# Softmax reciprocals brought into the attention's layout by VectorE block turns instead of TensorE transposes

## The reference

```python
x, ctx_1024: (8, 512, 512) float32
# attention, 16 heads of 32 columns, queries from layernorm(x), keys = values = ctx
scores = einsum('bhqd,bhkd->bhqk', qh, kh) / sqrt(32)
scores = where(|q - k| > 64, -inf, scores)        # a band of 64 keys to either side
attn = softmax(scores)
y = einsum('bhqk,bhkd->bhqd', attn, vh)           # heads joined again: (8, 512, 512)
x = x + y @ W_proj.T + b_proj
# gated recurrence over the 8 batch entries, on xn = layernorm(x)
for b in range(8):                                # xt = xn[b]: (512, 512), c: (512, 512)
    f = sigmoid(xt @ wf.T + c @ uf.T + bf)
    i = sigmoid(xt @ wi.T + c @ ui.T + bi)
    g = tanh(xt @ wc.T + c @ uc.T + bc)
    c = f * c + i * g
x = x + tanh(xn @ wo.T + c @ uo.T + bo)           # c of the last step for all b
```

## Time and profile before

| what | value |
|---|---|
| median of 3 runs (lowest, highest) | 1018.29 us (1018.28, 1021.04) |
| the profiled execution | 1014.17 us |
| its span, from first to last instruction | 1012.4 us |
| PE, PEld busy | 986.0 us (97%), 748.4 us (74%) |
| DVE busy | 605.5 us (60%) |
| ACT, POOL busy | 500.8 us (49%), 226.8 us (22%) |

### The profile page before, as it was taken

The page is one execution under the profiler, slowest core; times in us unless marked ns, Lnnn a source line. Parts: engine busy times, 40 slices in busy tenths (PEclk is TensorE's granted clock), DMA queues, the critical chain, the costliest instruction groups (busy, mean ns, idle before and its releaser), DMA issues.

```text
span 1012.4 us, 20358 instructions
## 1 busy us (share of the span) xinstructions
PE 986.0 (97%) x7100; PEld 748.4 (74%) x7100; DVE 605.5 (60%) x2194; ACT 500.8 (49%) x1472; POOL 226.8 (22%) x320
## 2 busy tenths in 40 slices
PE   6998999999999999999999999999999999999997
PEld 4664567777777777777777777777777778888886
DVE  5676887776567755776677656775586532133222
ACT  5767666555555445555455545455455432131221
POOL 4555322211111111211111111111121110002354
PEclk9998999999999999999999999999999999999999
DMA  8355322222222222211222222111111012029666
GB/s 268 123 153 177 110 74 79 84 79 74 80 84 79 74 70 67 71 46 63 78 85 80 73 80 84 58 53 48 61 38 50 11 39 108 0 99 360 247 218 198
DMA packets 76245, 99.37 MB, mean 98 GB/s; under 512 B 5232, under 2 KB 46192, under 8 KB 74608
## 3 DMA queue, kind: packets, MB, share of 16 engines
q1 hardware_dynamic: 75424, 97.80, 30.2%
q10 hardware_dynamic: 720, 0.27, 0.1%
HBM read 68.69 MB, written 29.36 MB: 97 GB/s over the span
## 4 chain that ended last, share of the span: by engine, by line
PE 87%; DMA 5%; DVE 2%; ACT 2%; issue 2%; POOL 1%; SPq 1%; DVEq 0%; POOLq 0%; ACTq 0%
PE ps_g L494 18%; PE ps_g L496 16%; PE ps_g L495 16%; PE ps_a L530 7%; PE ps_a L549 4%; PE ps_v L570 3%; PE ps_m L494 3%; PE ps_m L496 3%; PE ps_m L495 3%; PE ps_m L592 2%; PE ps_v L575 2%; ACT probs L670 1%; PE ps_m L604 1%; DMA keys<-x_dram 1%; PE ps_m L505 1%
## 5 line engine op out<-in xcount | busy, mean ns | idle before, releaser
L767 DVE CUSTOM_DVE_ANT_0 probs<-ps_a,mask 128x192 f32<-128x192 f32 (+1 forms) x512 | 169.5, 387 | 167.8 <-PE ps_a L530 158.8
L670 ACT ACTIVATE probs<-probs,rowmin 128x192 f32<-128x192 f32 (+1 forms) x512 | 239.2, 473 | 1.6 <-DVE rowmin L767 1.6
L712 ACT ACTIVATE gate<-ps_g,bias 128x512 f32<-128x512 f32 x84 | 57.8, 688 | 211.4 <-PE ps_g L496 211.4
L790 DVE STREAM_TRANSPOSE probs_t<-probs 32x128 f32<-32x128 f32 x492 | 146.5, 298 | 6.0
L478 POOL COPY recip<-invsum 128x128 f32<-128x128 f32 x128 | 37.7, 295 | 488.1 <-DVE invsum L774 488.1
L494 PE MATMUL ps_g<-state_hi,gate_w 128*128 128x512 f32 x336 | 138.2, 411 | 0.0
L675 ACT ACTIVATE probs_t<-ps_a 128x512 f32<-128x512 f32 x108 | 64.4, 596 | 147.4 <-PE ps_a L549 146.8
L496 PE MATMUL ps_g<-state_hi,gate_w 128*128 128x512 f32 x336 | 131.4, 391 | 0.0
L495 PE MATMUL ps_g<-state_lo,gate_w 128*128 128x512 f32 x336 | 131.3, 391 | 0.0
L670 ACT ACTIVATION_READ_ACCUMULATOR probs<-probs,rowmin 128x1 f32 x512 | 98.8, 193 | 0.0
L530 PE MATMUL ps_a<-keys,queries 32*128 32x256 f32 (+1 forms) x1024 | 86.2, 407 | 2.1 <-DVE rowmin L767 1.3
(11 more groups left out here) (177 smaller groups left out, 1764.6 us busy)
## 6 DMA issues: line engine op xcount, KB each, us to landing
values<-ctx_rows SPq DMA_DIRECT2D x34, 256.0 KB, 4.3
xr<-x SPq DMA_DIRECT2D x32, 256.0 KB, 3.9
keys<-ctx_t SPq DMA_DIRECT2D x16, 512.0 KB, 4.1
x_dram<-xr SPq DMA_DIRECT2D x32, 256.0 KB, 4.2
gate_w<-x2t_dram SPq DMA_DIRECT2D x8, 1024.0 KB, 10.9
keys<-ctx_t SPq DMA_DIRECT2D x16, 384.0 KB, 3.4
x2t_dram<-x2t_even SPq DMA_DIRECT2D x12, 512.0 KB, 4.0
x2t_dram<-x2t_odd SPq DMA_DIRECT2D x12, 512.0 KB, 3.8
```

Of the source, the lines that this page charges most:

```text
L670: act.activation(row, row, ACT.Exp, bias=rowmin[:, i % 2, h:h + 1], scale=-1.0, accum_out=rowsum[:, i // G % 2, i % G, h:h + 1]).then_inc( ...
L712: act.activation(gate[:, min(gt, 1), :], ps_g[i % 2][:, :], ACT.Tanh, bias=(first_bias if b == 0 else bias)[:, gt, m:m + 1], scale=1.0 if ...
L767: dve.tensor_tensor_reduce(probs[:, i % 2, h, 0:SEEN[t]], ps_a[h][:, 0:SEEN[t]], mask[:, MASK0[t]:MASK0[t] + SEEN[t]], -SCALE, -NEG, ALU.a ...
L790: turn = dve.transpose(probs_t[BLK * keys_of:BLK * (keys_of + 1), HPG:2 * HPG, q], probs[q, i % 2, :, col:col + BLK])
```

## The change

The step `spread` leaves TensorE, GpSimd and ScalarE and becomes VectorE's. For each half tile (two groups) it issues 16 block turns of a repeated column: for each of 4 heads and each of 4 blocks of 32 queries, 32 partitions of `invsum`, a column repeated 32 times for two groups, are turned into 32 partitions of `recip`. The half tile's `spread` stands behind `sides` in the slots with s of 0 and s of 2. `mult` reads `recip` as its second input and takes over two waits that `spread` had brought it before (for `tile_row` being free).

```diff
             if s > 0:
-                tile_steps((None, "query", "turn2", "spread")[s], (None, i + 1, i - 1, i)[s])
+                tile_steps((None, "query", "turn2", None)[s], (None, i + 1, i - 1, -1)[s])
             cells(2)
...
         if early:
-            tile_steps(("proj", "query", "turn2", "spread")[s], (i - 1, i + 1, i - 1, i)[s])
+            tile_steps(("proj", "query", "turn2", None)[s], (i - 1, i + 1, i - 1, -1)[s])
...
             steps.append(("recip", n + 1))
             if n + 1 >= OWN_BANKS:
                 steps.append(("sides", n + 1))
+            if (n + 1) % 2:
+                steps.append(("spread", (n + 1) // 2))
...
-                if kind == "recip":
-                    pool.wait_ge(inverted, i + 1)
-                    need(pool, spread, i // G)
-                    pool.tensor_copy(recip[:, i % G, :].rearrange("p (h d) -> p h d", h=HPG),
-                                     invsum[:, i // G % 2, i % G, :].unsqueeze(2).to_broadcast([P, HPG, HEAD]))\
-                        .then_inc(inv, 1)
...
-                if kind == "spread":
-                    pe.wait_ge(inv, G * (i + 1))
+                if kind == "proj":
                     need(pe, q_ready, min(i + 2, TILES))
                     need(pe, x2_lo, i)
-                    for g in range(G):
-                        mm = pe.transpose(ps_m[:, g * P:(g + 1) * P], recip[:, g, :], ident[:, :])
-                    mm.then_inc(spread, 1)
-                if kind == "proj":
...
-                if kind == "spread":
-                    act.wait_ge(spread, i + 1)
-                    act.activation(attn, ps_m[:, :].rearrange("p (g q) -> p g q", g=G), ACT.Copy).then_inc(recip_out, 1)
...
                 if kind == "recip":
                     r, g = i // G % 2, i % G
                     dve.wait_ge(expd, HPG * (i + 1))
-                    need(dve, inv, i - 2 * G + 1)
+                    need(dve, inv_turned, 2 * (i // G - 1))
                     dve.reciprocal(invsum[:, r, g, :], rowsum[:, r, g, :]).then_inc(inverted, 1)
+                if kind == "spread":
+
+                    tile, g0 = i // 2, 2 * (i % 2)
+                    dve.wait_ge(inverted, 2 * (i + 1))
+                    need(dve, attn_t, tile)
+                    for h in range(HPG):
+                        for c in range(0, P, BLK):
+                            sums = invsum[c:c + BLK, tile % 2, g0:g0 + 2, h:h + 1].to_broadcast([BLK, 2, HEAD])
+                            turn = dve.transpose(recip[HEAD * h:HEAD * (h + 1), g0:g0 + 2, c:c + BLK], sums)
+                    turn.then_inc(inv_turned, 1)
...
                 if kind == "mult":
-                    dve.wait_ge(recip_out, i + 1)
+                    dve.wait_ge(inv_turned, 2 * (i + 1))
                     dve.wait_ge(valued, G * (i + 1))
-                    dve.tensor_tensor(tile_row[:, :], ps_v[:, :], tile_row[:, :], ALU.mult).then_inc(attn_t, 1)
+                    dve.wait_ge(q_turned, min(i + 2, TILES))
+                    need(dve, x2_turned, i)
+                    dve.tensor_tensor(tile_row[:, :], ps_v[:, :], recip[:, :, :].rearrange("p g q -> p (g q)"),
+                                      ALU.mult).then_inc(attn_t, 1)
```

More of the change, by code:

```diff
@@ L290, in bass_xattn_ffn @@
         consts = sem("consts"); rstd1 = sem("rstd1"); rstd2 = sem("rstd2"); xr_ready = sem("xr_ready")
-        inv = sem("inv"); w_lo = sem("w_lo"); summed = sem("summed")
+        w_lo = sem("w_lo"); summed = sem("summed")
         attn_split = sem("attn_split"); wp_lo = sem("wp_lo")
         stat1 = sem("stat1"); aggr1 = sem("aggr1"); var1 = sem("var1"); ln1 = sem("ln1")
-        masked = sem("masked"); inverted = sem("inverted"); turned_b = sem("turned_b"); cleared = sem("cleared")
+        masked = sem("masked"); inverted = sem("inverted"); inv_turned = sem("inv_turned"); turned_b = sem("turned_b"); cleared = sem("cleared")
         attn_t = sem("attn_t"); x1_done = sem("x1_done")
@@ L300, in bass_xattn_ffn @@
         out_lo = sem("out_lo"); emptied_ps = sem("emptied_ps"); last_summed = sem("last_summed")
-        q_ready = sem("q_ready"); expd = sem("expd"); turned_a = sem("turned_a"); recip_out = sem("recip_out")
+        q_ready = sem("q_ready"); expd = sem("expd"); turned_a = sem("turned_a");
         attn_round = sem("attn_round"); wp_hi = sem("wp_hi")
@@ L307, in bass_xattn_ffn @@
         q_turned = sem("q_turned"); scored = sem("scored"); turned = sem("turned"); turned_2 = sem("turned_2"); valued = sem("valued")
-        spread = sem("spread"); projected = sem("projected"); state_used = sem("state_used")
+        projected = sem("projected"); state_used = sem("state_used")
         column = sem("column")
```

## The result

The changed kernel takes 1170.92 us (median of 4 runs, 1169.93 to 1171.87), the kernel before 1018.28 us (4 runs, 1017.36 to 1021.04): a ratio of 1.148, 95% interval 1.145 to 1.152. That is 153 us more, where 64 were forecast, and outside the range of 1041 to 1110. It lies even beyond the highest rival, 1127 us.

The account below looks back on a forecast made before the run. The prediction took TensorE as the bound before, with VectorE's work a floor under each stretch after. It added 15, 18 and 31 us to the profiled 1014.2, giving 1078, plus 4.1 for the runs' median: 1082 us, range 1041 to 1110.

Parts of the forecast that it names:

- the highest rival: Every burst: a turn costs by its count, not its size, 0.316 us, bursts of 5.05 us; 1127 us, chance 0.12.
- VectorE's total: Whole kernel: VectorE busy about 846 us, 79% of the span, with 1024 turns added to about 605 us.
- the worth of TensorE's saving taken alone: Whole kernel: 32 groups of four transposes leave TensorE, worth 14.8 us if TensorE is the bound everywhere.
- the chain through places 2 and 3: Six-cell slots: from place 2's masks to place 3's `value`, VectorE's work plus burst exceeds the time there; +31 us.
- At place 0 the burst lies beside the long projection: Six-cell slots, places 0 and 1: VectorE's lateness is worked off by the end of place 1; no time added.
- Not all of VectorE's waits for results there can be filled: Slots 0 to 19: 3 us of pauses on top of at least 12.3 us more; +15 us.
- some 0.2 us a slot: Slots 20 to 35: this much stays empty between dependent instructions, on top of +14.5 us; +18 us.
- The floors: VectorE's own work as each stretch's least length: 104.1 us in slots 0 to 19, 103.5 us in slots 20 to 35.
- The granted clock reads 1.00 there and 0.96 in slots 0 to 19: First 36 slots, "there" being slots 20 to 35: the clock was given no term, so no time.
- that only the averages count: Six-cell slots absorb the bursts, since a whole entry fits; only the first 36 slots pay; 1041 us, chance 0.14.
- That the load alone counts: Rival in the follow-up runs: only the amount of VectorE's work counts, wherever it stands; 1171 us for late0, no chance given.
- that turns aren't held: Every burst: turns not held up by partition changes, 0.135 us each, bursts of 2.2 us; 1023 us, chance 0.07.

Follow-up runs that it names:

- one_turn: Changed kernel with 15 of each burst's 16 turns left out, the rest of `recip` a constant: 1005.90 us, ratio 0.989 to the kernel before.
- late0: Changed kernel with the burst of place 0 moved behind `ln1b`, `resid` and `stat2` in slots 20 and later: 1118.19 us, ratio 1.098 to the kernel before.
- filled: Changed kernel with idle transposes on TensorE ahead of `value` in slots 0 to 19, where it waits: 1161.22 us, ratio 1.141 to the kernel before.
- late_all: As late0, and in slots 0 to 19 each burst also stands behind the next slot's copy: 1126.8 us, ratio 1.105 to the kernel before.
- wide_turns: Changed kernel with one burst a tile, at place 2, of 16 turns of 32 x 128 taking all four groups: 1135.91 us, ratio 1.116.
- one_block: Changed kernel with eight turns a burst, heads 2 and 3 left out, all reading and writing partitions 0 to 31: 1021.94 us, ratio 1.004.
- sides_first: As late0, with the blends of the gates behind `recip` and `sides` at place 3 of slots 20 and later: 1093.19 us, ratio 1.075.

## Why the prediction was wrong

The sign was right, and so were the price of a turn (0.248 us, bursts of 3.97; 0.248 and 3.98 measured), VectorE's total, the worth of TensorE's saving taken alone (14.8 us, 12 measured, by one_turn) and the chain through places 2 and 3. The four tiles' terms there, +3.1, +1.9, +0.65 and 0, came out as +3.2, +2.4, +1.0 and +0.2 in the entry from 515.94 us on. The six-cell slots miss 56 us, slots 0 to 19 21 us, slots 20 to 35 15 us. Three steps failed.

- *"At place 0 the burst lies beside the long projection, and VectorE's lateness is worked off by the end of place 1."* I walked VectorE's order and compared its lateness at the next masks, and left out that TensorE needs two of VectorE's results in between, though the same text names `query` as waiting for `ln1b` and `resid`. It could be seen in the trace of the kernel before. There `resid` ends at 421.12 us, 5.1 us after the masks' start, and TensorE's `query` starts at 422.47, 6.45 us after it: 1.35 us of slack for a burst of 3.97. That makes 2.6 us of wait, and 2.54 were measured. In the entry from 515.94 us on, places 0 and 1 of the four tiles cost 9.0 us, nothing was forecast. Moving the burst (late0) gave 53 us back. This is the largest part of the miss.
- *"Not all of VectorE's waits for results there can be filled; I take 3 us for those"*, and some 0.2 us a slot for slots 20 to 35. The floors held to 0.1 us in slots 0 to 19 and to 2 us in slots 20 to 35, and the time lay 24 and 21 us above them. In slots 0 to 19, 15.7 of the 23.9 us are waits that stay with the clock at its old value (filled), so the term of 3 us should have been near 16 of the 27 us in which VectorE was idle there. Neither another place (late_all) nor fewer, longer turns (wide_turns) made these slots shorter; the clock was low in both. In slots 20 to 35 late0 took 7 us off, so a third of the pause there came from the burst of place 0.
- *"The granted clock reads 1.00 there and 0.96 in slots 0 to 19, so it is no term here"*. That was the clock of the kernel before. Longer waits of TensorE gave half clock for 53 of the first 140 us. filled puts 8.6 us of slots 0 to 19 on it. In slots 20 to 35 (clock 0.89) its part wasn't separated from that of the waits. Nor do these runs say how much of the 15.7 us that are left in slots 0 to 19 belongs to which wait.

The rivals: that only the averages count (1041 us) is refuted by the entry itself, 127.1 us where the work of VectorE and of TensorE each fit into 109. That the load alone counts, the opposite, is refuted by late0: the same work, 8.7 us less. That a turn costs by its count is refuted by 236 ns against the 303 of wide_turns, and that turns aren't held by the 0.25 us from start to start and by one_block. The rival of 1127 us was nearest in number, but its condition, 0.316 us a turn, wasn't met.

## What to carry to other kernels

An engine at 60% has room for more work only where no other engine comes to wait for what stands behind that work. For each place of a moved block, list every consumer of every instruction behind the block up to the next one, and compare each with the time at which that consumer would be ready; the next wait of the engine itself isn't enough. Where two engines answer each other step by step, the idle time of one is in large part the working time of the other, and little of it can be filled: here 12 of 27 us, with the clock kept up. And where an insertion makes TensorE wait, the clock of the kernel before is no longer the clock of the kernel after.

## What the runs showed of the hardware

- A 32 x 64 float32 block turn starts 0.25 us after the last when it reads other 32 partitions than the last one (every fourth also writes others), 0.13 us after it when all read and write the same ones (one_block); the record of one is 236 and 190 ns long. A change of the output's partitions alone was not tried.
- A repeated column (stride 0) as a turn's input costs nothing that shows: 32 x 128 turns took 303 ns with it and 302 ns without.
- After waits of 2 to 6 us, TensorE's products ran at half clock for stretches. Idle transposes in the waits of slots 0 to 19 kept the clock up (0.96 against 0.79) and made the kernel faster, by 9.7 us in the changed kernel and by 11 us in sides_first.
- The time of one kernel scatters with the granted clock: ten runs of one_turn lay between 1004 and 1019 us, the fastest at a mean clock of 0.991, the slowest at 0.974.
